# GpSimd takes over three elementwise steps of a two-way decaying mix in front of a feed-forward kernel

## The chip, the cores and the metric

The kernel runs on one core of one Trainium2 chip. Its time is the device time of one execution, in microseconds (us). A core has five engines that run their own instruction queues beside each other and meet through semaphores: TensorE (PE, with its weight loads as PEld), VectorE (DVE), ScalarE (ACT), GpSimd (POOL) and SyncE (SP), which here only issues DMAs.

## The reference, cut to what matters

x and fside are 4 x 1024 (time) x 1024 (channels), float32. fside serves as k and v, x as r:

```
decay = exp(-exp(w)) * (0.5 + 0.5 * tf)          # one per batch and channel
ek, ekv = exp(min(k, 30)), exp(min(k, 30)) * v
a = a * decay + ek or ekv                        # over time, forward (nf, df) and reversed (nb, db)
euk = exp(min(u + k, 30))
num, den = nf + nb - ekv + euk * v, df + db - ek + euk
m = sigmoid(r) * num / max(den, 1e-8) * (0.8 + 0.2 * tf)
h = m @ W1.T                                     # 1024 -> 4096
a = gelu(clip(round(h / 0.1)) * 0.1)
out = x + a @ W2.T                               # 4096 -> 1024
```

## The kernel before, in words

The work is 8 blocks (`BLOCKS`): 4 batches of two time halves of 512 steps (`T`), the later half first. A block's mix is 8 tiles of 128 channels x 512 steps, numbered `g` over all blocks; `tile_of(g)` says whether it is of a late half. A block's feed-forward has a hidden stage of 8 steps (W1, quantise, gelu) and an output stage of 8 results of 128 channels (W2). Values go to TensorE as two float16 parts, a high part (ScalarE copies) and a low part (value minus high part). In block 0 the low parts are written by `mix_lo` (line 1034); later blocks have an operand scheme of their own (`operand_sums`, `operands_lo`), which the change does not touch.

Order of the work. The tiles of block 0 come first, alone (line 1124). Then, while TensorE does block n's feed-forward, the other engines make the tiles of block n+1, interleaved by hand: each engine's program is one fixed list, and `part(p, g)` (line 1015) is a quarter of a tile on VectorE. Tile g and tile g+2 share buffers (index `g % 2`).

A tile on VectorE: `weigh` makes ek * v. `forward` does two scans (NUM and DEN), `backward` two reversed ones into EK and EKV. `sums` adds: DEN + EK (line 992), the bonus terms (995, 998), NUM + EKV (1001, semaphore `s_num1`), the floor (1003), two 1-column carries, NUM + V (1009) and the gate (1012, `s_gate`). The reciprocal of the tile before (ScalarE's logarithm and exponential, two Newton steps and line 947) is woven into the scans.

A tile of a late half lacks the earlier half's state, so it is made directly: the exponent's argument is min(VP, 30) + RAMP * ln(decay) over the earlier half VP, ScalarE exponentiates and sums it, and `weigh` multiplies it by VP and sums (line 926, `s_dot`). The argument is `prefix_argument` (line 911): a one-input multiply (915) and a two-input instruction (918), both on VectorE, for tile g+1 after tile g's backward scans.

GpSimd only issues DMAs (line 446): in block 0's tiles one cast of a W1 piece per step to a float16 copy in memory (449, once the tile's R has landed) and every second step one of W2 (451); in block 0's hidden stage four more of W2, in its output stage three copies a step, each behind a semaphore of TensorE's progress. SyncE issues everything else in one list: `load_tile` loads VP, V and R, where VP waits for `s_dot` and V for `s_gate` of the tile two before; `ring_load` fills the ring of weights, where the first sixteen wait for the casts.

ScalarE waits for the argument (`s_arg`) in `exps`, for the floor in `reciprocal`, for the scaled output in `mix_hi`.

Of the kernel before, what the change touches and what calls it, by code (L numbers as in the profile page):

```python
# [6 lines left out]
ALU = mybir.AluOpType  # L7
# [8 lines left out]
CLIP = 30.0  # L16
# [17 lines left out]
def adaln_ffn_kernel(nc, x, fside, cond, w, u, w1, w2, out):  # L34
# [18 lines left out]
    with ExitStack() as ctx:  # L53
# [3 lines left out]
        def sem(name):  # L57
            return ctx.enter_context(nc.semaphore(name))
# [96 lines left out]
        s_vp = [sem(f"s_vp{k}") for k in range(2)]  # L155
        s_argr = sem("s_argr")
        s_arg = sem("s_arg")
        s_ekp = sem("s_ekp")
        s_dot = sem("s_dot")
        s_ekx = sem("s_ekx")  # L160
# [63 lines left out]
        def tile_of(g):  # L224

            n, t = g // CT, g % CT
            return n % BLOCKS // 2, n % 2 == 0, (t % 2) * KH + t // 2, CT * (n // 2) + t
# [216 lines left out]

        @block.gpsimd
        def _(pool):
            for s in range(STEPS):
                pool.wait_ge(s_r[s % 2], 16 * (s // 2 + 1))
                pool.dma_start(w1_half[s], w1_full[s]).then_inc(s_w1cast[s], 16)
                if s % 2 == 1:  # L450
                    pool.dma_start(w2_half[s // 2], w2_full[s // 2]).then_inc(s_w2cast[s // 2], 16)
            for d in range(DT // 2, DT):
                pool.wait_ge(s_h0, FPS * (d - 1))
                pool.dma_start(w2_half[d], w2_full[d]).then_inc(s_w2cast[d], 16)
            for s in range(STEPS):
                pool.wait_ge(s_y, 2 + s)
                pool.wait_ge(s_w1cast[s], 16)
                for r, h, k in ((WP1, 0, 0), (WP2, 0, 1), (WP4, 1, 1)):
                    pool.dma_start(w1s[s][:, r, :, :], w1_quads[s][:, h, :, k, :]).then_inc(s_w1copy[s], 16)
            for d in range(DT):  # L460
                pool.wait_ge(s_w2cast[d], 16)
            for s in range(STEPS):
                pool.wait_ge(s_w1copy[s], 16 * 3)

        @block.tensor
        def _(pe):
# [409 lines left out]
        def _(dve):  # L876
# [31 lines left out]
                dve.wait_ge(s_lndec, B + 1)  # L908
                dve.wait_ge(s_setup, 6 + B)

            def prefix_argument(g):
                b, late, c, pg = tile_of(g)
                if late:
                    dve.wait_ge(s_ramp, 3)
                    v.tensor_scalar(EKP[:, :], RAMP[:, :], lndec[:, b, c:c + 1], None, ALU.mult).then_inc(s_argr, 1)
                    dve.wait_ge(s_vp[pg % 2], 16 * (pg // 2 + 1))
                    dve.wait_ge(s_argr, pg + 1)
                    v.scalar_tensor_tensor(out=EKP[:, :], in0=VP[:, pg % 2, :], scalar=CLIP, in1=EKP[:, :],  # L918
                                           op0=ALU.min, op1=ALU.add).then_inc(s_arg, 1)

            def weigh(g):
                b, late, c, pg = tile_of(g)
                k = g % 2
# [64 lines left out]
            def sums(g):  # L988
                b, late, c, pg = tile_of(g)
                k = g % 2  # L990
                dve.wait_ge(s_dbwd, g + 1)
                v.tensor_tensor(DEN[:, k, :], DEN[:, k, :], EK[:, k, 1:T + 1], ALU.add).then_inc(s_den1, 1)
                dve.wait_ge(s_bon, g + 1)
                dve.wait_ge(s_vsq, g + 1)
                v.scalar_tensor_tensor(out=V[:, k, :], in0=BON[:, k, :], scalar=EXP_CLIP, in1=V[:, k, :],
                                       op0=ALU.min, op1=ALU.mult).then_inc(s_vbon, 1)
                dve.wait_ge(s_den1, g + 1)
                v.scalar_tensor_tensor(out=DEN[:, k, :], in0=BON[:, k, :], scalar=EXP_CLIP, in1=DEN[:, k, :],
                                       op0=ALU.min, op1=ALU.add).then_inc(s_den2, 1)
                dve.wait_ge(s_nbwd, g + 1)  # L1000
                v.tensor_tensor(NUM[:, k, :], NUM[:, k, :], EKV[:, k, 1:T + 1], ALU.add).then_inc(s_num1, 1)
                dve.wait_ge(s_den2, g + 1)
                v.tensor_scalar(DEN[:, k, :], DEN[:, k, :], DEN_MIN, None, ALU.max).then_inc(s_den3, 1)
                if late:
                    v.tensor_copy(carry[:, 0, c:c + 1], EKV[:, k, 0:1]).then_inc(s_carry, 1)
                    v.tensor_copy(carry[:, 1, c:c + 1], EK[:, k, 0:1]).then_inc(s_carry, 1)
                dve.wait_ge(s_num1, g + 1)
                dve.wait_ge(s_vbon, g + 1)
                v.tensor_tensor(NUM[:, k, :], NUM[:, k, :], V[:, k, :], ALU.add).then_inc(s_num2, 1)  # L1009
                dve.wait_ge(s_num2, g + 1)  # L1010
                dve.wait_ge(s_tanh, g + 1)
                v.scalar_tensor_tensor(out=NUM[:, k, :], in0=R[:, k, :], scalar=1.0, in1=NUM[:, k, :],
                                       op0=ALU.add, op1=ALU.mult).then_inc(s_gate, 1)

            def part(p, g):

                last = g - 1 if g % CT else None
                if p == 0:
                    weigh(g)
                if p == 1:  # L1020
                    forward(g, last)
                if p == 2:
                    backward(g, last)
                    if g % CT < CT - 1:
                        prefix_argument(g + 1)
                if p == 3:
                    sums(g)

            def divide(g):
                newton(g, 0)  # L1030
                newton(g, 1)
                mixed_out(g)

            def mix_lo(g):
                c = tile_of(g)[2]
                dve.wait_ge(s_mixhi, g + 1)
                v.tensor_tensor(mix0[:, c, 1, :], m_st[:, m_slot(g), g % 2, :], mix0[:, c, 0, :],  # L1037
                                ALU.subtract).then_inc(s_mix, 1)

            def operand_sums(n, q):  # L1040
                g, at = CT * n + 2 * q, KH * (n - 1) + q
# [78 lines left out]
                                       op0=ALU.mult, op1=ALU.not_equal, accum_out=bad[:, at:at + 1]).then_inc(s_chk, 1)  # L1120

            factors()
            prefix_argument(0)
            for t in range(CT):
                for p in range(4):
                    part(p, t)
                    if p == 3 and t > 0:
                        mix_lo(t - 1)
            divide(CT - 1)
            mix_lo(CT - 1)  # L1130

            def hidden_block0(g0):
                for s in range(STEPS):
# [17 lines left out]
            def hidden_block(n, nxt, g0):  # L1151
                for s in range(STEPS):
                    if nxt:
                        if s == 0:
                            prefix_argument(g0)
                        elif s % 2 == 0:
                            part(3, g0 + s // 2 - 1)
                        else:
                            part(1, g0 + s // 2)
                    if s >= 2:  # L1160
                        act_lo(n, s - 2, 1)
                    if s >= 1:
                        quantise22(n, s - 1)
                    if nxt:
                        part(0 if s % 2 == 0 else 2, g0 + s // 2)
                    seed_u4(n, s)
                    if s >= 1:
                        act_lo(n, s - 1, 0)
# [83 lines left out]
            def general_block(m):  # L1252
                n = BLOCKS + m
                for t in range(CT):
                    g = CT * n + t
                    prefix_argument(g)
                    weigh(g)
                    forward(g, None)
                    backward(g, None)
# [54 lines left out]
```

## Time and profile before

| | us |
|---|---|
| median of 3 runs (1815.62 to 1816.57) | 1816.48 |
| the profiled execution | 1813.9 |
| its span | 1811.6 |
| TensorE busy | 1699.9 (94%) |
| VectorE busy | 1279.5 (71%) |
| ScalarE busy | 1043.5 (58%) |
| GpSimd busy | 24.6 (1%) |

Busy time is an average over stages that have different limits; the table of stretches below shows it by stage. A wait counts the idle time of an engine in front of an instruction and names what came last. Idle time of an engine that is not the bottleneck costs nothing.

### The profile page before, as it was taken

To read this page: it belongs to the slowest core of one execution; us is meant where nothing else is said; L and a number is where in the kernel's file an instruction comes from. 1 tells how busy PE (TensorE), PEld (TensorE's weight loads), DVE (VectorE), ACT (ScalarE), POOL (GpSimd) and SP (SyncE) were. 2 spreads that over 40 slices of the span, in tenths; PEclk is the share of its full clock that TensorE was granted. 3 is DMA by queue.
4 is the path that set the end of the run, shared out by engine and by line. 5 is a ranking of instruction groups with operands and counts; after the bars stand their busy time and mean duration, and the time that the engine had idled before them with its cause. 6 is when DMAs were issued, how large, how long until landed. Compare 5 with 4: busy or idle time off the path is not lost. (4 is left out here: it accounts for less than half of the span.)

```text
span 1811.6 us, 27451 instructions
## 1 busy us (share of the span) xinstructions
PE 1699.9 (94%) x10882; PEld 1067.0 (59%) x10882; DVE 1279.5 (71%) x2008; ACT 1043.5 (58%) x1422; POOL 24.6 (1%) x44
## 2 busy tenths in 40 slices
PE   1459999999999999999999999999999999999998
PEld 0124434687448854588447864488545874478643
DVE  8988885878866786779866777678966687633211
ACT  5458843687437863498526874388634885255300
POOL 0000021000000000000000000000000000000000
PEclk9679999999999999999999999999999999999999
DMA  8747785665546644655446545466445654365442
GB/s 239 178 128 204 253 286 198 204 198 181 162 147 204 195 139 155 198 191 202 162 133 203 187 158 174 144 217 204 156 144 192 195 180 152 120 194 158 145 129 82
DMA packets 109238, 321.16 MB, mean 177 GB/s; under 512 B 12720, under 2 KB 12720, under 8 KB 108592
## 3 DMA queue, kind: packets, MB, share of 16 engines
q1 hardware_dynamic: 106416, 296.28, 50.1%
q0 software_dynamic: 2688, 23.07, 5.5%
q8 instruction: 87, 1.43, 0.3%
q14 instruction: 47, 0.39, 0.1%
HBM read 310.91 MB, written 48.23 MB: 198 GB/s over the span
## 5 line engine op out<-in xcount | busy, mean ns | idle before, releaser
L562 PE MATMUL ps<-act,w_ring 128*128 128x512 f16 x4096 | 890.7, 380 | 4.4 <-DVE y_out L1111 4.4
L506 PE MATMUL ps<-mo,w_ring 128*128 128x256 f16 x6272 | 690.6, 273 | 11.0 <-ACT ps L706 6.1
L562 PEld LDWEIGHTS ps<-act,w_ring 128*128 128x128 f16 x4096 | 401.4, 98 | 485.7 <-issue 8.8
L506 PEld LDWEIGHTS ps<-mo,w_ring 128*128 128x128 f16 x6272 | 612.5, 98 | 90.1 <-issue 7.8
L1102 DVE SCALAR_TENSOR_TENSOR act<-a,act 128x1024 f16<-128x1024 f32 x128 | 156.2, 1221 | 134.7 <-ACT act L755 134.7
L1111 DVE SCALAR_TENSOR_TENSOR y_out<-ps,x_in 128x512 f32<-128x512 f32 x64 | 44.1, 690 | 175.1 <-PE ps L562 107.3
L763 ACT ACTIVATE q<-chk_full 128x1024 int8<-128x1024 f32 x64 | 67.0, 1047 | 144.5 <-DMA chk_full<-in_w_dram 144.5
L749 ACT ACTIVATE a<-q 128x1024 f32<-128x1024 int16 x128 | 135.3, 1057 | 14.6 <-DVE act L1102 10.3
L755 ACT ACTIVATE act<-a 128x1024 f16<-128x1024 f32 x128 | 134.2, 1049 | 0.9
L483 PE MATMUL ps<-mo,w_ring 128*128 128x512 f16 x128 | 42.6, 509 | 89.3 <-DVE mo L1037 89.3
L1119 DVE SCALAR_TENSOR_TENSOR chk_full<-q,chk_full 128x1024 f32<-128x1024 int8 x64 | 78.1, 1220 | 43.8 <-ACT q L763 43.8
L696 ACT ACTIVATE mo<-a 128x1024 f16<-128x1024 f32 x28 | 29.6, 1057 | 128.8 <-DVE a L1048 128.8
L650 ACT ACTIVATE EK<-V 128x512 f32<-128x512 f32 x64 | 39.9, 623 | 109.6 <-DMA V<-in_fside_dram 109.3
L646 ACT ACTIVATE EKP<-EKP 128x512 f32<-128x512 f32 x32 | 20.2, 631 | 133.7 <-DVE EKP L918 133.5
L1085 DVE SCALAR_TENSOR_TENSOR ps<-sp,ps 128x512 f32<-128x512 f32 x56 | 38.8, 692 | 73.7 <-PE ps L506 66.9
L483 PEld LDWEIGHTS ps<-mo,w_ring 128*128 128x128 f16 x128 | 15.4, 125 | 116.0 <-issue 55.8
L496 PE MATMUL ps<-mo,w_ring 128*128 128x512 f16 x384 | 83.0, 379 | 0.0
L670 ACT ACT_TABLE_LOAD x64 | 82.1, 1283 | 1.1
L643 ACT ACT_TABLE_LOAD x64 | 82.1, 1283 | 1.1
L733 ACT ACTIVATE q<-ps 128x512 int16<-128x512 f32 x56 | 33.3, 594 | 85.6 <-PE ps L506 85.6
L978 DVE TENSOR_TENSOR_SCAN EK<-EK,decay 128x512 f32<-128x512 f32 x64 | 81.7, 1277 | 0.1
L983 DVE TENSOR_TENSOR_SCAN EKV<-EKV,decay 128x512 f32<-128x512 f32 x64 | 81.6, 1276 | 0.0
(94 smaller groups left out, 1461.1 us busy)
## 6 DMA issues: line engine op xcount, KB each, us to landing
w_ring<-w1s SPq DMA_DIRECT2D x168, 512.0 KB, 3.7
w_ring<-w_half SPq DMA_DIRECT2D x144, 512.0 KB, 4.2
chk_full<-in_w_dram SPq DMA_DIRECT2D x64, 512.0 KB, 4.6
V<-in_fside_dram SPq DMA_DIRECT2D x64, 256.0 KB, 4.7
R<-in_x_dram SPq DMA_DIRECT2D x64, 256.0 KB, 4.8
w_half<-in_w_dram POOLq DMA_DIRECT2D x16, 1024.0 KB, 7.9
x_in<-in_x_dram SPq DMA_DIRECT2D x64, 256.0 KB, 5.3
out_dram<-y_out SPq DMA_DIRECT2D x64, 256.0 KB, 4.8
```

The source lines that it names most:

```text
L496: mm = pe.matmul(bank[4 * (s % 2) + j][:, :], w1_ring[:, k, f, c, :], mix0[:, c, p, :], start=(c == 0 and p == 0), stop=(c == CT - 1 and p ...
L506: mm = pe.matmul(dst[:, f, :], wp_ring[:, k, r, f, q, :], mo[:, op, q, p, :], start=(fresh and f == 0 and q == 0 and p == 0), stop=(q == K ...
L562: mm = pe.matmul(y_ps[y][:, :], w2_ring[:, k, f, :], act[:, a, p, :], start=(a == 0 and p == 0), stop=(a == FT - 1 and p == 1))
L643: sc.preload_act_table_set(EXP_SET)
L670: sc.activation(R[:, g % 2, :], R[:, g % 2, :], ACT.Tanh, scale=0.5).then_inc(s_tanh, 1)
L749: sc.activation(a32[:, 2 * h:2 * h + 2, :], q16[:, s % 2, 2 * h:2 * h + 2, :], ACT.Gelu_apprx_tanh, scale=QSTEP).then_inc(s_gelu, 1)
L755: sc.activation(act[:, f:f + 2, 0, :], a32[:, 2 * h:2 * h + 2, :], ACT.Copy, scale=ACT_SCALE).then_inc(s_ahi, 1)
L763: sc.activation(chk_i8, chk_full[:, :], ACT.Copy, scale=W_SCALE).then_inc(s_chki8, 1)
L978: v.tensor_tensor_scan(EK[:, k, 0:T][:, ::-1], EK[:, k, 0:T][:, ::-1], dec(b, c), EK[:, k, T:T + 1], ALU.add, ALU.mult).then_inc(s_dbwd, 1)
L983: v.tensor_tensor_scan(EKV[:, k, 0:T][:, ::-1], EKV[:, k, 0:T][:, ::-1], dec(b, c), EKV[:, k, T:T + 1], ALU.add, ALU.mult).then_inc(s_nbwd, 1)
L1102: v.scalar_tensor_tensor(out=act[:, f:f + 2, 1, :], in0=a32[:, 2 * h:2 * h + 2, :], scalar=ACT_SCALE, in1=act[:, f:f + 2, 0, :], op0=ALU.m ...
L1119: v.scalar_tensor_tensor(out=chk_full[:, :], in0=chk_i8, scalar=1.0 / W_SCALE, in1=chk_full[:, :], op0=ALU.mult, op1=ALU.not_equal, accum_ ...
```

## The change

Three steps move from VectorE's list to GpSimd's.

1. The exponent's argument of each late tile. On GpSimd it is three instructions instead of two: the multiply, the minimum into the tile's BON buffer (which is free until ScalarE's exponential fills it), and the sum. It now waits for `s_dot` of the late tile before and for `s_gate` of the tile two before.
2. The add of the backward numerator, NUM + EKV, of every tile, right behind `s_nbwd`.
3. The low part of block 0's tiles (`mix_lo`).

They stand between GpSimd's DMA issues as the diff shows. The fallback path behind the last If gets them too; it is not taken with these inputs.

```diff
@@ GpSimd's program
+            def prefix_argument(g):
+                b, late, c, pg = tile_of(g)
+                if late:
+                    pool.wait_ge(s_ramp, 3)
+                    pool.wait_ge(s_lndec, B + 1)
+                    if pg > 0:
+                        pool.wait_ge(s_dot, pg)
+                    pl.tensor_scalar(EKP[:, :], RAMP[:, :], lndec[:, b, c:c + 1], None, ALU.mult).then_inc(s_argr, 1)
+                    pool.wait_ge(s_vp[pg % 2], 16 * (pg // 2 + 1))
+                    pool.wait_ge(s_argr, pg + 1)
+                    if g >= 2:
+                        pool.wait_ge(s_gate, g - 1)
+                    pl.tensor_scalar(BON[:, g % 2, :], VP[:, pg % 2, :], CLIP, None, ALU.min).then_inc(s_kp, 1)
+                    pool.wait_ge(s_kp, pg + 1)
+                    pl.tensor_tensor(EKP[:, :], BON[:, g % 2, :], EKP[:, :], ALU.add).then_inc(s_arg, 1)
+
+            def mix_lo(g):
+                c = tile_of(g)[2]
+                pool.wait_ge(s_mixhi, g + 1)
+                pl.tensor_tensor(mix0[:, c, 1, :], m_st[:, m_slot(g), g % 2, :], mix0[:, c, 0, :],
+                                ALU.subtract).then_inc(s_mix, 1)
+
+            def add_backward(g):
+                k = g % 2
+                pool.wait_ge(s_nbwd, g + 1)
+                pl.tensor_tensor(NUM[:, k, :], NUM[:, k, :], EKV[:, k, 1:T + 1], ALU.add).then_inc(s_num1, 1)
+
+            prefix_argument(0)
             for s in range(STEPS):
                 pool.wait_ge(s_r[s % 2], 16 * (s // 2 + 1))
                 pool.dma_start(w1_half[s], w1_full[s]).then_inc(s_w1cast[s], 16)
+                if s + 1 < CT:
+                    prefix_argument(s + 1)
                 if s % 2 == 1:
                     pool.dma_start(w2_half[s // 2], w2_full[s // 2]).then_inc(s_w2cast[s // 2], 16)
+                add_backward(s)
+                if s > 0:
+                    mix_lo(s - 1)
+            mix_lo(CT - 1)
             for d in range(DT // 2, DT):
                 pool.wait_ge(s_h0, FPS * (d - 1))
                 pool.dma_start(w2_half[d], w2_full[d]).then_inc(s_w2cast[d], 16)
+                add_backward(CT + d - DT // 2)
             for s in range(STEPS):
...
+                if s % 2 == 1:
+                    add_backward(CT + CT // 2 + s // 2)
+            for g in range(2 * CT, CT * BLOCKS):
+                if g % CT == 0 and g > 2 * CT:
+                    add_backward(g - 1)
+                prefix_argument(g)
+                if g % CT > 0:
+                    add_backward(g - 1)
+            add_backward(CT * BLOCKS - 1)
...
@@ VectorE's program: prefix_argument, mix_lo and all calls of them are gone, and in sums
-                dve.wait_ge(s_nbwd, g + 1)
-                v.tensor_tensor(NUM[:, k, :], NUM[:, k, :], EKV[:, k, 1:T + 1], ALU.add).then_inc(s_num1, 1)
```

## Rows read from the trace of the kernel before

**Rows 1.** stretches: length, busy us of PE, PEld, DVE, ACT, POOL; clock, DMA share, GB/s.

```profile
40.00:80.00 40.00, 15.75 (x44) 5.37 (x42) 39.31 (x70) 18.64 (x34) 2.44 (x5) 0.68 0.80 178
...
600.00:800.00 200.00, 199.68 (x1330) 129.82 (x1328) 146.33 (x221) 121.93 (x164) 0.00 (x0) 1.00 0.55 177
```

**Rows 2.** waits up to 134 us: who waited for whom, total us, times, longest.

```profile
POOL w_half L449 <- DMA R<-in_x_dram: 93.1, 8, 19.4
PE ps L483 <- DVE mo L1037: 89.3, 7, 37.8
...
ACT EKP L646 <- DVE EKP L918: 46.0, 8, 7.1
```

**Rows 3.** VectorE, one tile of the front: start us, us, engine, line, operation.

```profile
99.71 0.69 DVE L937 TENSOR_TENSOR DEN<-DEN,RCP 128x512 f32<-128x512 f32 x1
...
102.09 1.28 DVE L983 TENSOR_TENSOR_SCAN EKV<-EKV,decay 128x512 f32<-128x512 f32 x1
103.29 0.73 DVE L947 SCALAR_TENSOR_TENSOR m_st<-NUM,ogain_neg,RCP 128x512 f32<-128x512 f32 x1
103.93 0.48 DVE L915 TENSOR_SCALAR EKP<-RAMP,lndec 128x512 f32<-128x512 f32 x1
104.52 0.69 DVE L918 SCALAR_TENSOR_TENSOR EKP<-VP,EKP 128x512 f32<-128x512 f32 x1
105.13 0.68 DVE L992 TENSOR_TENSOR DEN<-DEN,EK 128x512 f32<-128x512 f32 x1
...
106.93 0.69 DVE L1001 TENSOR_TENSOR NUM<-NUM,EKV 128x512 f32<-128x512 f32 x1
107.53 0.42 DVE L1003 TENSOR_SCALAR DEN<-DEN 128x512 f32<-128x512 f32 x1
...
108.00 0.68 DVE L1009 TENSOR_TENSOR NUM<-NUM,V 128x512 f32<-128x512 f32 x1
...
109.32 0.69 DVE L1037 TENSOR_TENSOR mo<-m_st,mo 128x512 f16<-128x512 f32 x1
109.92 0.69 DVE L926 SCALAR_TENSOR_TENSOR EKV<-EKP,VP 128x512 f32<-128x512 f32 x1
...
114.18 0.69 DVE L937 TENSOR_TENSOR DEN<-DEN,RCP 128x512 f32<-128x512 f32 x1
```

**Rows 4.** all engines, the first tile's argument and the first casts.

```profile
7.44 0.65 POOL L449 DMA_DIRECT2D w_half<-in_w_dram  x1 [6.99 <-DMA R<-in_x_dram]
...
8.85 0.49 DVE L915 TENSOR_SCALAR EKP<-RAMP,lndec 128x512 f32<-128x512 f32 x1
...
9.65 0.51 POOL L449 DMA_DIRECT2D w_half<-in_w_dram  x1 [1.56 <-DMA R<-in_x_dram]
...
10.18 0.63 ACT L646 ACTIVATE EKP<-EKP 128x512 f32<-128x512 f32 x1 [0.94 <-DVE EKP L918]
...
15.89 0.45 SPq L315 DMA_DIRECT2D VP<-in_fside_dram  x1
```

**Rows 5.** VectorE, the last two low parts of the front.

```profile
122.60 0.69 DVE L1037 TENSOR_TENSOR mo<-m_st,mo 128x512 f16<-128x512 f32 x1
...
126.77 0.69 DVE L1037 TENSOR_TENSOR mo<-m_st,mo 128x512 f16<-128x512 f32 x1 [0.70 <-ACT mo L681]
```

**Rows 6.** TensorE, first matmul group behind the first result of block 0.

```profile
246.87 15.34 PE L562 MATMUL ps<-act,w_ring 128*128 128x512 f16 x57 [4.44 <-DVE y_out L1111]
```

**Rows 7.** waits of TensorE after the front.

```profile
PE ps L506 <- ACT ps L706: 6.1, 7, 1.3
PE ps L506 <- DVE mo L1054: 4.5, 4, 1.6
```

**Rows 8.** VectorE, a hidden stage of block 1.

```profile
395.51 1.23 DVE L1102 SCALAR_TENSOR_TENSOR act<-a,act 128x1024 f16<-128x1024 f32 x1 [3.75 <-ACT act L755]
...
419.96 1.22 DVE L1102 SCALAR_TENSOR_TENSOR act<-a,act 128x1024 f16<-128x1024 f32 x1 [3.75 <-ACT act L755]
```

**Rows 9.** waits of VectorE after the front.

```profile
DVE y_out L1111 <- PE ps L562: 102.6, 20, 12.0
```

More of the change, by code:

```diff
@@ L157, in adaln_ffn_kernel @@
         s_arg = sem("s_arg")
+        s_kp = sem("s_kp")
         s_ekp = sem("s_ekp")
@@ L446, in _ @@
         def _(pool):
+            pl = nc.gpsimd
+            def prefix_argument(g):
[23 more added lines that the diff above has]
+            prefix_argument(0)
             for s in range(STEPS):
@@ L463, in _ @@
                 pool.wait_ge(s_w1copy[s], 16 * 3)
+            pool.wait_ge(s_flag, 1)
+            needs_general = pool.value_load(flag[0:1, 0:1], min_val=0, max_val=1)
+            with pool.If(needs_general > 0):
+                for g in range(CT * BLOCKS, 2 * CT * BLOCKS):
+                    prefix_argument(g)
+                    add_backward(g)
         @block.tensor
@@ L909, in factors @@
                 dve.wait_ge(s_setup, 6 + B)
[L911 to L919, printed above, removed]
             def weigh(g):
@@ L1023, in part @@
                     backward(g, last)
-                    if g % CT < CT - 1:
-                        prefix_argument(g + 1)
                 if p == 3:
@@ L1032, in divide @@
                 mixed_out(g)
[L1034 to L1038, printed above, removed]
             def operand_sums(n, q):
@@ L1122, in _ @@
             factors()
-            prefix_argument(0)
             for t in range(CT):
@@ L1126, in _ @@
                     part(p, t)
-                    if p == 3 and t > 0:
-                        mix_lo(t - 1)
             divide(CT - 1)
-            mix_lo(CT - 1)
             def hidden_block0(g0):
@@ L1153, in hidden_block @@
                     if nxt:
-                        if s == 0:
-                            prefix_argument(g0)
-                        elif s % 2 == 0:
+                        if s % 2 == 1:
+                            part(1, g0 + s // 2)
+                        elif s > 0:
                             part(3, g0 + s // 2 - 1)
-                        else:
-                            part(1, g0 + s // 2)
                     if s >= 2:
@@ L1255, in general_block @@
                     g = CT * n + t
-                    prefix_argument(g)
                     weigh(g)
```

## The prediction, made before the changed kernel was run

> **What bounds the kernel now.** I read the table of stretches first [rows 1]. In the steady part (600 to 800 us) TensorE is busy 199.7 of 200 us; between 40 and 80 us it is busy 15.8 of 40 while VectorE is busy 39.3. So there are two kernels in one: a front that ends near 127 us, in which VectorE paces the eight tiles of block 0, and the long rest, in which TensorE does. The waits of the front say the same [rows 2]: TensorE waited 89.3 us for the low part that VectorE writes on line 1037. ScalarE waited 46.0 us for the exponent's argument, so ScalarE is not the pace. GpSimd waited 93.1 us for loads and is otherwise empty. After the front all waits of TensorE sum to 15.0 us (4.4 + 6.1 + 4.5) [rows 6, 7]. Whatever the change does to the time, it does in the front, or by making VectorE late enough later on to open new gaps in TensorE.
>
> VectorE's queue of one tile is the unit of the sum [rows 3]. Line 937 starts at 99.71 and again at 114.18: a tile takes 14.47 us, back to back. I count start to start, since the ends overlap the next start by some 0.08 us.
>
> **Removed from VectorE, per tile.** The argument (lines 915 and 918): 103.93 to 105.13, 1.20 us. The backward numerator's add (line 1001): 106.93 to 107.53, 0.60 us. The low part (line 1037): 109.32 to 109.92, 0.60 us. In all 2.40 of 14.47 us.
>
> In the front that is 7 arguments (tiles 1 to 7), 8 adds and 6 low parts (tiles 0 to 5; tile 6's lay in VectorE's wait for ScalarE at the end, and tile 7's ends the front): 8.4 + 4.8 + 3.6 = 16.8 us removed.
>
> **Moved to the ends of the front.** Argument 0 runs from 8.85 until ScalarE takes it at 10.18 [rows 4]; as three instructions instead of two, on GpSimd, it ends some 0.8 us later. Low part 7 is the last thing before TensorE's sixteen final matmuls of the stage [rows 5]: 126.77 plus 0.69 us now, some 0.5 us longer on a slower engine. Low part 6, which now waits its turn until 122.60, can be made as soon as ScalarE has copied the high part, but TensorE then only has its sixteen matmuls done earlier and waits for tile 7; no gain.
>
> **Price of an instruction on GpSimd.** The trace has no GpSimd instruction that reads a tile; its only work is issuing DMAs at 0.49 us. Lower bound: what VectorE takes, 0.48 us for one input and 0.60 for two. Upper bound: the slowest row of this shape, the scan, 1.20 us start to start [rows 3]. For one input I take 0.48, for two 1.20, because GpSimd has to fetch two tiles and no row suggests it does so as fast as the engine built for it. By the Trainium skill (GPSIMD Engine Reference, Elementwise — side-by-side cycle accounting) an add of 2048 elements takes 1.96 times as long on GpSimd; as an estimate that would be 1.18 us here, and the sum would be the same.
>
> **Does that time lie beside VectorE's?** This decides the sign. Nothing in the trace shows both engines reading tiles at once, so both ends stand. What rows do show: VectorE's one-input instruction on line 1003 (0.42 us) handles the same 512 elements that the two-input ones take 0.68 us for [rows 3]. An engine that goes about twice as fast with one input uses both of its read paths for it; with two inputs both are taken as well. Nearly everything in its queue (scans, products, sums) has two tile inputs. If GpSimd has no path of its own, its reads have to take VectorE's. I therefore put the likelier case at "they take turns", each GpSimd instruction holding back the VectorE one behind it for its whole length.
>
> The Trainium skill (SBUF — State Buffer, Who interferes with whom) has this as a rule: a VectorE instruction with two SBUF inputs contends with a GpSimd instruction that reads SBUF, and the second to issue waits in full. No run so far shows it; by it the sum is the one for turns below, without it the one for side by side.
>
> Taking turns, the front changes by: arguments 7 x (0.48 + 0.48 + 1.20 - 1.20) = +6.7; argument 0 +0.8; adds 8 x (1.20 - 0.60) = +4.8; low parts 6 x 0.60 = +3.6; low part 6 now competes with tile 7's sums, +1.2; low part 7 +0.5. Together +17.6 us. From it goes what VectorE can do while GpSimd holds the path: the small memsets and carry copies and the accumulator read, some 0.5 us a tile, 3.5 us in seven tiles. Front: +14.1 us.
>
> **Waits that are added.** Line 1009 now waits for GpSimd's add. The backward scan ends near 103.3 (line 947 starts behind it at 103.29), line 1009 starts at 108.00, or 106.2 with the argument and the add gone: 2.9 us of cover for a 1.20 us instruction. It does not bind unless the add takes over 2.8 us. Behind it on VectorE stand lines 1012 and the next tile's product. The argument is needed only by the next tile's product, 10 us later, so its chain of three is covered.
>
> **GpSimd's own queue.** Each weight cast now stands behind an argument, an add and a low part, so casts 1 to 7 start up to 10 us later relative to R's landing. The sync engine's ring loads wait for them in order, and tile loads stand behind those. The first casts now start near 11 us instead of 7.44 and 19 instead of 9.65 [rows 4]; VP of tile 2 would then be issued near 20 instead of 15.9 and is needed after 22. I cost this at nothing; if the cover is gone it is a few us once, in tiles 1 and 2.
>
> **After the front.** In block 0's hidden stage VectorE is nearly full, and its lateness shows once: TensorE waits 4.4 us for the first result on line 1111 [rows 6]. Two adds (tiles 10 and 11) lie in the unbroken run before it: 2 x 0.60 less if side by side, 2 x 0.60 more if in turns, so +1.2. In the hidden stages of later blocks VectorE waits 3.75 us for ScalarE in every two steps (24.5 us) [rows 8]; the extra per late tile in turns is 0.96 + 0.60 = 1.6 us, which fits. TensorE's other waits stay [rows 7]: 6.1 us are for ScalarE's copy, which the change does not touch. The output stages have VectorE waiting for TensorE for 102.6 us in all [rows 9]. The other 24 arguments and most of the 56 later adds lie where TensorE does not wait for VectorE, and gain or lose nothing.
>
> **Sum.** The profiled run took 1813.9 us (span 1811.6). Plus 14.1 and 1.2 is 1829.2. The median of the runs lies 2.6 us above the profiled run, so 1831.8 us.
>
> **Rivals.**
> 1. Side by side (ends faster). GpSimd reads without holding VectorE back. Front -16.8 + 0.8 + 0.5 = -15.5; block 0 -1.2. 1797.2, with the offset 1799.8 us. For it: GpSimd's DMA issues lie in VectorE's full queue without a stretched instruction beside them; against it: those do not read tiles, and the pair 0.42 against 0.68. It decides from any price up to 2.8 us, since covered work costs nothing.
> 2. In turns, but GpSimd is as quick as VectorE (0.48 and 0.60). Arguments 7 x 0.36 = +2.5, ends +1.3, low part 6 +0.6, less 3.5 of small work: about +1. 1817 us; a half-way overlap of slow instructions ends in the same place (1808 to 1824).
> 3. A two-input instruction takes over 2.4 us when it has to fight for the path. Then line 1009 waits, the extra per late tile passes the 3.75 us of slack, and TensorE gets gaps in 24 late tiles: over 1850 us. Nothing in the rows speaks for it.
> The change does what it says: the instructions are really gone from VectorE's queue, so "nothing happens" is only rival 2.
>
> **Chances.** Turns 0.52, side by side 0.30, rival 2 0.10, rival 3 0.08. What this kernel's measurement can tell from no change is 0.2%, 3.6 us. Faster: 0.30 plus a part of rival 2, 0.33; within: 0.09; slower: 0.58. The range takes in side by side at its near half (1799) and ends where turns with every instruction in full, 17.6 in the front, and some late gaps end (1843). The likeliest case alone runs from 1822 to 1843.
>
> **What would show each step.** VectorE's rows in the front: two-input instructions that stretch from 0.68 us beside a GpSimd one (turns), or keep their 0.68 (side by side). The tile's period, 14.47 us now: 16 with turns, 12.1 side by side. Mean of the GpSimd add: 1.2 us. Line 1009's wait for GpSimd: none. TensorE's wait on line 483: 89.3 us growing to some 103, or falling to 74. TensorE's wait for line 1111: 5.6 or 3.2 us. I am wrong if VectorE's instructions keep their lengths, or if the time moves outside the front.

## The result and the profile after

| | before | after |
|---|---|---|
| median (range, runs), us | 1816.05 (1814.51 to 1816.57, 4) | 1842.42 (1842.04 to 1842.82, 4) |
| ratio, 95% interval | | 1.0147 [1.0129, 1.0164] |
| profiled execution / its span | 1813.9 / 1811.6 | 1842.8 / 1840.9 |
| TensorE / VectorE / ScalarE / GpSimd busy | 1699.9 / 1279.5 / 1043.5 / 24.6 | 1708.8 / 1281.3 / 1045.9 / 325.4 |

The median of before now takes in a fourth run. The changed kernel is slower, by 26.4 us in the medians and by 29.3 us in the spans of the two profiled executions (the one of before lay 2.1 us under its median). VectorE gave away 136 of its 2008 instructions and is no less busy: 1281.3 against 1279.5 us. Its remaining instructions became longer.

I read first where TensorE's stages start, since their distance is the loss of each stage. The front's end is the first matmul on line 550 (before: line 496); a block's output stage begins with its unbroken run of 448 matmuls on line 616 (before: 562).

| start of | before | after | later by | added here |
|---|---|---|---|---|
| block 0's hidden stage | 131.76 | 142.55 | 10.8 | 10.8 |
| block 1's output stage | 447.72 | 463.50 | 15.8 | 5.0 |
| block 7's output stage | 1707.65 | 1733.49 | 25.8 | 10.0 |
| VectorE's last instruction | 1806.34 | 1832.18 | 25.8 | 0 |
| end of the span | 1811.6 | 1840.9 | 29.3 | 3.5 |

So four places carry it: the front 10.8, the way from block 0 to block 1 5.0, blocks 1 to 7 10.0, and what lies behind the last instruction 3.5 us.

**The front.** The two stretches after, in the columns of [rows 1]:

```profile
40.00:80.00 40.00, 17.59 (x48) 6.07 (x48) 39.41 (x56) 20.12 (x30) 27.42 (x18) 0.79 0.74 165
600.00:800.00 200.00, 199.21 (x1322) 128.94 (x1320) 150.46 (x217) 120.41 (x160) 25.29 (x14) 1.00 0.54 172
```

VectorE is still full in the front (39.4 of 40 us) with 56 instructions in place of 70, and TensorE now loses something in the steady part too. TensorE's waits over the whole run, against [rows 2, 7]:

```profile
PE ps L537 <- POOL mo L469: 53.2, 6, 10.5
PE ps L537 <- DMA w_ring<-w_half: 44.4, 1, 44.4
PE ps L560 <- DVE mo L1088: 9.4, 6, 2.4
PE ps L560 <- DVE y_out L1145: 7.2, 4, 4.9
```

The wait of this stage is now 53.2 + 44.4 = 97.6 us in place of 89.3. The first wait ended at 44.41 with the ring's load; the first low part had been written at 41.13 (line 469, 39.80 plus 1.33). So 3.3 us of it are the late weight casts. They cost nothing in the end, since the next groups of matmuls wait for low parts again. The same tile-long piece of VectorE's list as in [rows 3], from line 975 to line 975:

```profile
90.04 1.06 DVE L975 TENSOR_TENSOR EKV<-EK,V 128x512 f32<-128x512 f32 x1
...
92.40 1.56 DVE L1005 TENSOR_TENSOR_SCAN DEN<-decay,pre_d,EK 128x512 f32<-128x512 f32 x1
93.91 1.76 DVE L981 TENSOR_TENSOR DEN<-DEN,RCP 128x512 f32<-128x512 f32 x1
...
101.12 1.20 DVE L1045 TENSOR_SCALAR DEN<-DEN 128x512 f32<-128x512 f32 x1
...
102.37 1.52 DVE L1051 TENSOR_TENSOR NUM<-NUM,V 128x512 f32<-128x512 f32 x1
...
105.59 1.06 DVE L975 TENSOR_TENSOR EKV<-EK,V 128x512 f32<-128x512 f32 x1
```

and GpSimd in the same stretch:

```profile
89.87 1.56 POOL L457 TENSOR_SCALAR EKP<-RAMP,lndec 128x512 f32<-128x512 f32 x1 [1.55 <-DVE EKV L970]
91.59 2.18 POOL L462 TENSOR_SCALAR BON<-VP 128x512 f32<-128x512 f32 x1
93.85 1.26 POOL L464 TENSOR_TENSOR EKP<-BON,EKP 128x512 f32<-128x512 f32 x1
...
98.73 3.31 POOL L475 TENSOR_TENSOR NUM<-NUM,EKV 128x512 f32<-128x512 f32 x1 [3.07 <-DVE EKV L1027]
102.00 1.33 POOL L469 TENSOR_TENSOR mo<-m_st,mo 128x512 f16<-128x512 f32 x1
```

Put side by side, each GpSimd instruction has one stretched VectorE instruction beside it: 975 takes 1.06 instead of 0.69 us, 1005 1.56 instead of 1.26, 981 1.76 instead of 0.69, 1045 1.20 instead of 0.42, 1051 1.52 instead of 0.68. The two beside one-input instructions (457, 462) lost 0.37 and 0.30 (and line 462 itself took 2.18 us instead of the 1.49 it takes alone), the three beside two-input ones (464, 475, 469) 1.07, 0.78 and 0.84: together 3.36 us. Removed were 2.40, and 0.11 us is a new gap in front of line 1045. The period is 105.59 - 90.04 = 15.55 us, 1.08 more than in [rows 3]; 3.36 + 0.11 - 2.40 = 1.07. From the first tile's line 975 (14.91, before: line 931 at 12.00) to the eighth's (121.15, before: 110.99) the changed kernel loses 7.25 us: 0.74 in the first step and 1.08 in each of the six others. The last tile and its low part add 0.6. The rest of the front's 10.8 is its beginning:

```profile
8.38 1.57 POOL L457 TENSOR_SCALAR EKP<-RAMP,lndec 128x512 f32<-128x512 f32 x1 [7.94 <-DVE lndec L961]
10.11 1.49 POOL L462 TENSOR_SCALAR BON<-VP 128x512 f32<-128x512 f32 x1 [0.16 <-POOL EKP L457]
11.68 1.26 POOL L464 TENSOR_TENSOR EKP<-BON,EKP 128x512 f32<-128x512 f32 x1
```

The first argument ends at 12.94 us, against 10.14 before although it starts earlier [rows 4], and VectorE's first product starts at 13.84 instead of 10.93: 2.9 us later. These rows also give GpSimd's prices with VectorE idle: 1.57 and 1.49 us for one input, 1.26 for two.

**From block 0 to block 1.** GpSimd after:

```profile
293.64 1.51 POOL L475 TENSOR_TENSOR NUM<-NUM,EKV 128x512 f32<-128x512 f32 x1 [7.72 <-DVE EKV L1027]
295.09 4.12 POOL L497 DMA_DIRECT2D w1s<-w_half  x6
```

and before, the last of these copies:

```profile
284.74 2.05 POOL L459 DMA_DIRECT2D w1s<-w_half  x3 [4.86 <-PE ps L562]
```

Six copies of weights stood 7.72 us behind tile 14's add, which waited for VectorE's backward scan. SyncE's ring load of those weights was issued at 303.61 instead of 289.86, and the loads of V, R and x_in stand behind it in SyncE's list. VectorE felt it (first row), then TensorE (the other two):

```profile
309.28 0.69 DVE L1145 SCALAR_TENSOR_TENSOR y_out<-ps,x_in 128x512 f32<-128x512 f32 x1 [15.08 <-DMA x_in<-in_x_dram]
...
345.71 1.44 PE L560 MATMUL ps<-mo,w_ring 128*128 128x256 f16 x6 [4.88 <-DVE y_out L1145]
349.57 43.42 PE L560 MATMUL ps<-mo,w_ring 128*128 128x256 f16 x378 [2.42 <-DVE mo L1088]
```

Before, TensorE waited 1.59 and 1.28 us at the same seam, the passage from one block's output stage to the next block's hidden stage (at 335.03 and 339.59), so the seam's longer waits are 4.4 of the 5.0 us. During the first of them the granted clock falls to 0.50, the lower of its two levels (1.2 GHz), and stays there from 343.4 to 353.7.

The stall behind the first result of block 0, 4.44 us in [rows 6], is now 3.21. A second one, of 1.20 us, stands at 326.86, in front of the block's eighth result. It belongs to the copies' delay, since the run that undoes that delay (e4 below) doesn't have it.

**From block to block.** From one output stage's start to the next the six stretches add 2.3, 2.1, 1.8, 1.8, 1.9 and 0.3 us. GpSimd makes two arguments in the first, third and fifth, six in the second and fourth, and none in the last, so the drift stands where arguments are made. I followed it in the first, at the end of block 1's output stage. The chain is long. Before:

```profile
503.53 0.43 SPq L315 DMA_DIRECT2D VP<-in_fside_dram  x1
...
507.31 0.69 DVE L918 SCALAR_TENSOR_TENSOR EKP<-VP,EKP 128x512 f32<-128x512 f32 x1 [7.43 <-DMA VP<-in_fside_dram]
...
508.03 0.63 ACT L646 ACTIVATE EKP<-EKP 128x512 f32<-128x512 f32 x1 [17.58 <-DVE EKP L918]
...
515.59 1.23 DVE L1119 SCALAR_TENSOR_TENSOR chk_full<-q,chk_full 128x1024 f32<-128x1024 int8 x1 [1.12 <-ACT q L763]
...
518.17 0.43 SPq L329 DMA_DIRECT2D x_in<-in_x_dram  x1
...
524.06 0.69 DVE L1111 SCALAR_TENSOR_TENSOR y_out<-ps,x_in 128x512 f32<-128x512 f32 x1 [4.24 <-DMA x_in<-in_x_dram]
```

After:

```profile
519.31 0.43 SPq L316 DMA_DIRECT2D VP<-in_fside_dram  x1
...
523.46 1.49 POOL L462 TENSOR_SCALAR BON<-VP 128x512 f32<-128x512 f32 x1 [15.25 <-DMA VP<-in_fside_dram]
525.03 1.27 POOL L464 TENSOR_TENSOR EKP<-BON,EKP 128x512 f32<-128x512 f32 x1
...
526.34 0.63 ACT L700 ACTIVATE EKP<-EKP 128x512 f32<-128x512 f32 x1 [17.00 <-POOL EKP L464]
...
533.10 1.23 DVE L1153 SCALAR_TENSOR_TENSOR chk_full<-q,chk_full 128x1024 f32<-128x1024 int8 x1 [2.61 <-ACT q L817]
...
535.68 0.43 SPq L330 DMA_DIRECT2D x_in<-in_x_dram  x1
...
541.68 0.69 DVE L1145 SCALAR_TENSOR_TENSOR y_out<-ps,x_in 128x512 f32<-128x512 f32 x1 [4.35 <-DMA x_in<-in_x_dram]
```

VP's load is issued 15.8 us later in both, which is the lateness that was there already. From its landing to ScalarE's exponential it is 0.72 us before and 2.88 after. Of this 2.16 us more, ScalarE had 0.87 to spare, which it spent waiting for the floor before. Its list carries the rest on to its next quantising step, VectorE's check waits 2.61 instead of 1.12 us for that, SyncE's load of the next piece waits for the check, x_in stands behind it, and y_out waits for x_in: 17.6 us later where VP was 15.8 later. What TensorE then does:

```profile
561.21 0.82 PE L560 MATMUL ps<-mo,w_ring 128*128 128x256 f16 x6 [0.85 <-DVE y_out L1145]
564.00 93.79 PE L560 MATMUL ps<-mo,w_ring 128*128 128x256 f16 x842 [1.98 <-DVE mo L1088]
```

From one output stage's start to the next (block 1's to block 2's) the stretches are, before and then after, in the columns of [rows 1]:

```profile
447.70:658.70 211.00, 208.89 (x1411) 137.57 (x1410) 157.32 (x245) 130.99 (x177) 0.00 (x0) 1.00 0.53 173
```

```profile
463.50:676.70 213.20, 210.37 (x1411) 138.29 (x1409) 153.85 (x232) 131.08 (x177) 22.91 (x15) 0.99 0.54 171
...
566.00:572.00 6.00, 6.00 (x44) 4.67 (x43) 2.73 (x5) 4.92 (x7) 0.00 (x0) 0.78 1.00 377
```

Of the 2.2 us that this block adds, 0.7 are TensorE's longer idle time (2.83 for 2.11 us) and 1.5 are the same 1411 matmuls taking longer. The last row shows where: behind the two waits of 0.85 and 1.98 us the granted clock is 0.78 of full speed in the mean over 6 us, in which TensorE is never idle. For 3.4 us (565.3 to 568.7) it stands at its lower level, 1.2 GHz. The same happens at the seams behind blocks 3 and 5, and at none behind blocks 2, 4 and 6. It isn't a second price, though. In e1 below, which keeps the arguments on GpSimd, the clock does not fall here and the stretch adds 2.0 us all the same (212.95 us, TensorE busy 208.99), now all of it idle time:

```profile
557.26 3.28 PE L536 MATMUL ps<-mo,w_ring 128*128 128x256 f16 x26 [1.99 <-DVE mo L1072]
561.56 89.24 PE L536 MATMUL ps<-mo,w_ring 128*128 128x256 f16 x816 [1.03 <-ACT ps L736]
```

The slower matmuls take the place of the third wait. Over the whole run TensorE is busy 8.9 us longer for the same instructions, at a mean granted clock of 0.976 instead of 0.982; how much of that is lost time isn't shown.

In the stretches with six arguments most of the loss lies in the hidden stage. From block 2's output stage to block 3's TensorE waits 0.62 us at the seam (before: 0.32) and 0.39 and 0.42 us for VectorE's quantising step (line 1129), and the same 1411 matmuls take 209.30 instead of 208.48 us at full clock. The chain of these was not followed.

There is a rival at the seam. GpSimd's add stands in its list behind an argument that waits for VP, and VectorE waits for the add: 2.90 us at 502.36 and 5.36 us at 527.39 (line 1051), and likewise in blocks 3 and 5. e1 has these arguments and no add on GpSimd, and the first stretch adds 2.0 there as against 2.3. So it is the argument and not the add that carries most of the drift.

**Behind the last instruction.** VectorE's last instruction (line 1278) starts at 1832.18 and the span ends 8.7 us later; before it was 5.3 us (1806.34 to 1811.6).

### The profile page after: what moved, and what is told of

It is laid out like the page before. It is cut to its first block and busy times, and to the rows that moved or that the text cites. A ratio compares the mean times of both kernels' runs of the same rounds, so it can differ in the third digit from the quotient of the medians.

```text
span 1840.9 us, 27520 instructions
## 1 busy us (share of the span) xinstructions
PE 1708.8 (93%) x10882; PEld 1069.7 (58%) x10882; DVE 1281.3 (70%) x1872; ACT 1045.9 (57%) x1422; POOL 325.4 (18%) x212
## 5 line engine op out<-in xcount | busy, mean ns | idle before, releaser
L560 PE MATMUL ps<-mo,w_ring 128*128 128x256 f16 x6272 | 699.1, 274 | 19.7 <-DVE mo L1088 9.4
L560 PEld LDWEIGHTS ps<-mo,w_ring 128*128 128x128 f16 x6272 | 615.4, 98 | 105.1 <-issue 15.3
L475 POOL TENSOR_TENSOR NUM<-NUM,EKV 128x512 f32<-128x512 f32 x64 | 134.1, 2095 | 869.8 <-DVE EKV L1027 869.8
L1136 DVE SCALAR_TENSOR_TENSOR act<-a,act 128x1024 f16<-128x1024 f32 x128 | 162.4, 1269 | 137.9 <-ACT act L809 137.9
L537 PE MATMUL ps<-mo,w_ring 128*128 128x512 f16 x128 | 45.0, 531 | 97.7 <-POOL mo L469 53.2
L462 POOL TENSOR_SCALAR BON<-VP 128x512 f32<-128x512 f32 x32 | 62.1, 1942 | 171.2 <-DMA VP<-in_fside_dram 169.7
L457 POOL TENSOR_SCALAR EKP<-RAMP,lndec 128x512 f32<-128x512 f32 x32 | 52.8, 1651 | 194.3 <-DVE EKV L970 186.3
```

The source lines that it names most:

```text
L462: pl.tensor_scalar(BON[:, g % 2, :], VP[:, pg % 2, :], CLIP, None, ALU.min).then_inc(s_kp, 1)
L475: pl.tensor_tensor(NUM[:, k, :], NUM[:, k, :], EKV[:, k, 1:T + 1], ALU.add).then_inc(s_num1, 1)
L537: mm = pe.matmul(bank[4 * s + j][:, :], w1_ring[:, slots[2 * s + j // 2], j % 2, c, :], mix0[:, c, p, :], start=(t == 0 and p == 0), stop= ...
L560: mm = pe.matmul(dst[:, f, :], wp_ring[:, k, r, f, q, :], mo[:, op, q, p, :], start=(fresh and f == 0 and q == 0 and p == 0), stop=(q == K ...
L1136: v.scalar_tensor_tensor(out=act[:, f:f + 2, 1, :], in0=a32[:, 2 * h:2 * h + 2, :], scalar=ACT_SCALE, in1=act[:, f:f + 2, 0, :], op0=ALU.m ...
```

## The experiments

Each ratio is against runs of the kernel before that were taken along with it (medians 1815.4 to 1815.5, for the changed kernel 1816.05). "Front" is the start of block 0's hidden stage less 131.76.

| run | median, us | ratio, 95% | front | block 1 / 7 later by | tail, us |
|---|---|---|---|---|---|
| changed kernel | 1842.42 | 1.0147 [1.0129, 1.0164] | +10.8 | 15.8 / 25.8 | 8.7 |
| e1 argument only | 1832.96 | 1.0100 [1.0083, 1.0117] | +6.2 | 9.0 / 18.0 | 5.6 |
| e2 additions only | 1820.92 | 1.0028 [1.0017, 1.0039] | +3.6 | 7.3 / 9.6 | 5.5 |
| e3 low parts only | 1815.25 | 0.9996 [0.9986, 1.0006] | +1.2 | 4.1 / 5.0 | 5.0 |
| e4 copies first | 1837.91 | 1.0120 [1.0103, 1.0137] | +10.9 | 11.1 / 20.7 | 8.6 |
| e5 before + reading probe | 1836.76 | 1.0116 [1.0100, 1.0131] | +21.0 | 24.0 / 24.6 | 5.4 |
| e6 before + writing probe | 1816.42 | 1.0005 [0.9996, 1.0015] | +0.5 | 1.8 / 3.0 | 5.1 |
| e7 branch on VectorE | 1840.25 | 1.0132 [1.0117, 1.0148] | +10.2 | 16.9 / 26.6 | 5.1 |
| e8 ScalarE's product | 1811.33 | 0.9979 [0.9970, 0.9988] | -3.4 | -4.3 / -3.5 | 5.3 |
| e9 late arguments back | 1829.50 | 1.0077 [1.0060, 1.0094] | +10.7 | 13.3 / 15.6 | 5.4 |

The block columns come from single profiled executions, and the stall behind block 0's first result alone moves them by some 3 us. It also shows a pattern: 4.4 to 7.8 us in the six kernels in which VectorE makes the adds (before, e1, e3, e5, e6, e8), 2.2 to 3.3 in the five in which GpSimd does (changed, e2, e4, e7, e9). The front and the drift from block 1 to 7 are steadier.

**e1, e2, e3: one part at a time.** The changed kernel with two of its three moves undone.

```
e1   (GpSimd)   prefix_argument kept; mix_lo and add_backward back on VectorE
e2   (GpSimd)   add_backward kept; prefix_argument and mix_lo back on VectorE
e3   (GpSimd)   mix_lo kept; the other two back on VectorE, and no branch at GpSimd's end
```

> Only the exponent's argument is on GpSimd; the add and the low part are on VectorE. Theory (a GpSimd instruction that reads tiles holds back the VectorE instruction behind it): VectorE's product on line L975 and its scan and product behind it stretch by 0.37, 0.31 and 1.07 us a tile, 1.75 against 1.20 saved, +0.55 us in 7 tiles, and the first argument comes 3.5 us later: front +7.4 us. With the tail's 3.4 us and some later gaps 1827 to 1835 us. Rival (VectorE is late because it waits for GpSimd's result): the argument is needed only 10 us later, so nothing stretches, front -8.4 + 3.5 = -5 us, about 1815 us with the tail.

> Only the add of the backward numerator is on GpSimd. Theory: GpSimd gets at its tiles only when VectorE leaves a gap, and then the one-input floor instruction stretches from 0.42 to 1.20 us: +0.78 + 0.11 - 0.60 = +0.3 us a tile, front +2.3 us; in block 0's output stage the adds stand before the copies of weights, +5.6 us; tail +3.4 us. 1826 to 1834 us. Rival (waits): VectorE idles in front of the line that adds V, and the rows there show it.

> Only the low part of block 0 is on GpSimd, and there is no If in GpSimd's program. Theory: +0.83 - 0.60 = +0.23 us a tile in six, +0.5 at the end: front +2 us, nothing later, no longer tail: 1817 to 1820 us. Rival (side by side): front -3.6 + 0.5 = -3 us, 1813 us.

Measured: 1832.96, 1820.92 and 1815.25 us. The fronts add up (6.2 + 3.6 + 1.2 = 11.0 against 10.8). The argument is the dearest part: it brings two one-input instructions, a two-input one and the late start. VectorE in e1, a tile:

```profile
87.33 1.06 DVE L951 TENSOR_TENSOR EKV<-EK,V 128x512 f32<-128x512 f32 x1
...
91.20 1.76 DVE L957 TENSOR_TENSOR DEN<-DEN,RCP 128x512 f32<-128x512 f32 x1
...
102.36 1.06 DVE L951 TENSOR_TENSOR EKV<-EK,V 128x512 f32<-128x512 f32 x1
```

The same three are stretched by the same amounts (line 951 by 0.37, the scan 1.56 instead of 1.26, line 957 by 1.07); the period is 15.03 us. They are the argument's. e1 also keeps 9.0 of the 10.0 us that blocks 1 to 7 add; e2 has 2.3 and e3 0.9 of it.

e2 came out 5 us under its expectation. Its front lost more than expected (3.6 against 2.3 us), the way to block 1 less (3.7 against 5.6), and the 3.4 us behind the last instruction did not come (5.5 against 5.3 us before). Nor is it the floor that stretches in e2 (0.43 us) but the multiply of the argument, a one-input instruction too, which VectorE still makes there: 1.32 instead of 0.48 us (line 935 at 90.72). e1's tail did not come either (5.6 us).

e3 came out under its expectation as well and is indistinguishable from before: GpSimd takes the low part while VectorE runs a scan, which goes from 1.28 to 1.99 us, so 0.71 is paid for 0.60 removed.

**e4: the weight copies ahead of tiles 14 and 15's adds.**

```
-                if s % 2 == 1:
+                if s in (1, 3):
                     add_backward(CT + CT // 2 + s // 2)
+            add_backward(2 * CT - 2)
+            add_backward(2 * CT - 1)
```

> The changed kernel with the adds of tiles 14 and 15 moved behind GpSimd's last weight copies. Theory: in block 0's output stage the copies stood behind an add that waits for VectorE, SyncE's list stood behind the copies, and results and tile loads behind SyncE: 15.1 us of VectorE's wait for x_in, seen by TensorE as 5.6 us more of gaps. They go: 1835 to 1838 us. Rival (those gaps are VectorE's stretched instructions): no change, 1842 us.

1837.91 us, 4.5 less than the changed kernel. Block 1's output stage starts 4.7 us earlier (458.82), block 7's 5.1 us. TensorE waits 0.24 and 3.04 us at the seam instead of 4.88 and 2.42, and not at all in front of block 0's eighth result. That settles the second place: the copies' delay was worth 4.5 to 5 us, and it was only an order in one list. (The two ratios' intervals overlap; all four runs of e4, 1834.4 to 1838.8, lie under all four of the changed kernel.)

**e5, e6: is it reading?** Both put five idle instructions per tile of the front beside the unchanged kernel's VectorE, at the places where the change has its own. In e5 they read (two one-input, three two-input, all into scratch), in e6 they are memsets of the same tile, which read nothing.

```
+            def extra(two_inputs):
+                pool.wait_ge(s_scr, done[0])
e5+              pl.tensor_tensor(SCR, RAMP, RAMP, ALU.add)  or  pl.tensor_scalar(SCR, RAMP, CLIP, None, ALU.min)
e6+              pl.memset(SCR, 1.0)
```

> The kernel before, with five more GpSimd instructions per tile of block 0 at the places of the change (two with one input, three with two inputs, all from a constant tile into an unused buffer); VectorE keeps all its instructions and nobody waits for the new ones. Theory (reads on GpSimd hold VectorE back): VectorE's instructions stretch by about 3.4 us a tile, front +20 to +25 us, 1836 to 1842 us. Rival (what costs is waiting for GpSimd's results): nothing stretches, 1816 us.

> As the run that adds reads, but the five extra instructions are memsets of the same size: they write a tile and read none. Theory (it is the reading that collides): no stretch beside VectorE's two-input instructions, 1816 to 1818 us. Rival (any GpSimd instruction on tiles collides): +10 us or more.

e5 took 1836.76 us, e6 1816.42. Three of the five stretched rows of VectorE in e5:

```profile
92.14 1.41 DVE L1039 SCALAR_TENSOR_TENSOR NUM<-R,NUM 128x512 f32<-128x512 f32 x1
...
97.43 1.57 DVE L988 TENSOR_TENSOR_SCAN DEN<-decay,pre_d,EK 128x512 f32<-128x512 f32 x1
98.93 1.52 DVE L964 TENSOR_TENSOR DEN<-DEN,RCP 128x512 f32<-128x512 f32 x1
```

Stretched are line 1039 by 0.72, 988 by 0.31, 964 by 0.83, and 942 by 0.78 and 958 by 0.29: 2.93 us a tile, and seven tiles of that are 20.5 of the front's 21.0. In e6 the same rows keep their length beside the memsets:

```profile
99.10 1.26 DVE L988 TENSOR_TENSOR_SCAN DEN<-decay,pre_d,EK 128x512 f32<-128x512 f32 x1
100.30 0.69 DVE L964 TENSOR_TENSOR DEN<-DEN,RCP 128x512 f32<-128x512 f32 x1
```

```profile
96.79 1.32 POOL L460 MEMSET chk_full<- 128x512 f32 x2 [0.38 <-DVE EKV L953]
```

The waits and semaphores of the two probes are the same. The memsets are shorter, five of them some 2.6 us a tile; had they held VectorE back for that length, the front would be 18 us later, as an estimate, and it is 0.5 later. So no dependence, queue or semaphore stretches VectorE's rows; GpSimd's reading does. The Trainium skill (SBUF — State Buffer, Who interferes with whom) says the same of two-input VectorE instructions, and that GpSimd instructions which only write don't contend: both agree with these runs. Its "fully blocks" comes near for GpSimd's two-input instructions (0.71 to 1.07 us lost beside 1.26 us of work), and does not hold for its one-input ones (0.29 to 0.37 lost beside 1.5).

**e7: where does the tail come from?** GpSimd's branch, which holds the general path's arguments and adds and is never taken, is removed, and VectorE's own branch, which is there in every kernel, makes them as before.

```
-            pool.wait_ge(s_flag, 1)
-            needs_general = pool.value_load(flag[0:1, 0:1], min_val=0, max_val=1)
-            with pool.If(needs_general > 0):
-                ...
```

> The changed kernel with the never-taken fallback of the three steps in VectorE's If and none in GpSimd's program. Theory: the 3.4 us between the last VectorE instruction and the end of the span that the changed kernel has more than before (8.7 against 5.3 us) belong to GpSimd's branch; they go: 1839 us. Rival: the tail has another cause and stays, 1842.4 us.

1840.25 us; the tail is 5.1 us, 3.6 less. The spans differ by 2.9 us, as block 7 is 0.8 later here, and the medians by 2.2 (the ratios' intervals overlap, the two sets of runs don't). So the tail belongs to the branch, although it does nothing. Having a branch on GpSimd is not enough: e1, e2 and e9, whose branch holds only the arguments or only the adds, end after 5.4 to 5.6 us. Why the whole body costs over 3 us and either half next to nothing is not shown.

**e8: the multiply on ScalarE.** The kernel before, with the one-input product of tiles 1 to 7 made by ScalarE, which waited 46.0 us for it [rows 2].

```
+            def product(g):
+                act_e.wait_ge(s_dot, pg)
+                sc.activation(EKP[:, :], RAMP[:, :], ACT.Copy, scale=lndec[:, b, c:c + 1]).then_inc(s_argr, 1)
```

> The kernel before, with the product RAMP * ln(decay) of tiles 1 to 7 made by ScalarE, which waits 46 us in the front, in place of VectorE (one 0.48 us instruction per tile, 0.58 us start to start). Theory (ScalarE does not slow VectorE): front 7 x 0.58 = 4.1 us shorter, 1812 us. Rival (the product comes late, as ScalarE is behind): same or slower, 1816 to 1819 us.

1811.33 us: faster than both kernels, by 4.1 us (0.2%). The front is 3.4 us shorter. VectorE after its reciprocal's last step goes straight on to the sum; the tile's period is 13.88 us (line 936 from 91.93 to 105.81), 0.59 less than in [rows 3], and nothing in it is stretched:

```profile
99.77 0.72 DVE L957 SCALAR_TENSOR_TENSOR m_st<-NUM,ogain_neg,RCP 128x512 f32<-128x512 f32 x1
100.41 0.68 DVE L928 SCALAR_TENSOR_TENSOR EKP<-VP,EKP 128x512 f32<-128x512 f32 x1
...
105.81 0.69 DVE L936 SCALAR_TENSOR_TENSOR EKV<-EKP,VP 128x512 f32<-128x512 f32 x1
```

**e9: the drift of the later blocks.** The changed kernel with the arguments of blocks 2, 4 and 6 on VectorE again.

```
             for g in range(2 * CT, CT * BLOCKS):
-                prefix_argument(g)
+    (VectorE)   prefix_argument(g), two instructions, in its old place, for g >= 2 * CT
```

> The changed kernel, with the argument of the tiles of blocks 2, 4 and 6 made on VectorE again, in its old two instructions and its old place; block 0's arguments, the low parts and all additions stay on GpSimd. Theory (the later blocks' drift of 10 us is the price of the late arguments: the argument alone on GpSimd showed 9.0 of it, the additions alone 2.3): the front stays 10 to 11 us late, block 1's product as late as in the changed kernel (463 us), but from there to block 7 it loses at most 3 us instead of 10, and the tail shrinks by 1 us or more since the branch's body is smaller: 1829 to 1834 us. Rival: the drift comes from the additions' waits and the later clock dips, and stays: 1840 to 1843 us. If the tail's 3.4 us come from the size of the branch's body, it is between 5.5 and 8.7 us here.

1829.50 us, 12.9 less than the changed kernel. The front is as late as there (142.49), blocks 1 to 7 add 2.3 us instead of 10.0, and the tail is 5.4 us. At the seam followed above, VP's landing and ScalarE's exponential are 0.72 us apart again:

```profile
520.97 0.69 DVE L970 SCALAR_TENSOR_TENSOR EKP<-VP,EKP 128x512 f32<-128x512 f32 x1 [6.93 <-DMA VP<-in_fside_dram]
...
521.69 0.63 ACT L698 ACTIVATE EKP<-EKP 128x512 f32<-128x512 f32 x1 [17.28 <-DVE EKP L970]
```

and VectorE's check waits 1.12 us for ScalarE as it did before the change (line 1163 at 528.77); TensorE is busy 208.88 us in that block, as before. So the late arguments carry 7.7 of the 10.0 us. They also bring VectorE's wait for the add, which is gone in e9 too; that this is not what costs is e1's to say, as above. The spans of the two profiled executions differ by 13.5 us; the rest of that is the tail (3.3 us, with only the adds in the branch) and 2.4 us between the front and block 1's output stage, where block 2's first arguments are made, and where single executions differ by as much.

## Why the prediction was right in sign and short in size

1832 us was forecast, in turns, with a range to 1843; 1842.4 was measured, at its edge. The sign and the mechanism of the front held. But of 29.3 us only 10.8 lie in the front. The prediction had named time that moves outside the front as a sign of being wrong, and by that sign its account of the rest was wrong: 18.5 us came from places that it costed at 1.2. That the time still fell inside the range is in part luck. Step by step:

- **"In turns" is the case.** Two-input instructions stretched beside GpSimd's (0.69 to 1.76 us), and e5 against e6 shows that it is the reading. The period was to be 16 us with turns and is 15.55. Side by side (12.1 us), rival 1, is out.
- **The price of an instruction.** Two inputs: 1.20 taken, 1.26 measured alone, and 0.78 to 1.07 of it lost by VectorE. One input: 0.48 taken, 1.49 to 1.57 measured, but only 0.30 to 0.37 lost. The row I leaned on for one input was VectorE's own lower bound. For VectorE both errors are on the same side: 4.56 us a tile less the 0.5 allowed for small work was forecast, 3.36 measured. The front came out 10.8 us late where 14.1 was forecast. The 0.5 us a tile of small work that was to go on beside GpSimd was not measured by itself.
- **Argument 0: 0.8 us forecast, 2.9 measured.** Here the one-input price counts in full, since nothing runs beside it. It hides a part of the overestimate above.
- **The add's mean of 1.2 us is wrong: 2.10,** 3.31 in the front. It does not run slowly; it doesn't get in. Line 475 was released by the scan at 98.6 and VectorE's next four instructions followed one another without a stretch until the short gap in front of line 1045 (101.12), where GpSimd began and VectorE waited. So its release took three times its length, and still line 1051 did not wait in the front, as forecast (though not for the forecast's reason, a limit of 2.8 us: the stretched line 1045 moved line 1051 back with it). In later blocks it waited six times, 24.7 us in all, the longest 5.4, each time because the add stood behind an argument that waited for VP. This is rival 3's place; e1, which has no such wait, drifts by 9.0 us all the same.
- **TensorE's wait on the low parts: 103 forecast, 97.6 measured,** of which 3.3 are for the ring's load.
- **Behind block 0's first result: 5.6 forecast, 3.21 measured.** Here the sign was wrong. 3.2 is what the prediction gave for side by side, yet line 1045 is stretched to 1.20 us in this stage too (at 239.61). All five kernels with the adds on GpSimd have this stall at 2.2 to 3.3 us; why it shortens was not followed.
- **"GpSimd's own queue costs nothing" failed.** I followed it for the casts, where it was right in the outcome (the first group of matmuls waited 3.3 us for them, the front's end did not move), and not for the weight copies of block 0's output stage, which are the same queue 170 us later. 5 us (e4 recovered 4.5).
- **"After the front nothing" failed.** I compared VectorE's extra work (1.6 us a tile) with its idle 3.75 us in the hidden stages [rows 8], and that slack held only for the most part: in block 3's hidden stage TensorE waited 0.39 and 0.42 us for VectorE. The output stages were waved through with VectorE's 102.6 us of waiting [rows 9]. But the argument is there not VectorE's work but a link between a load and ScalarE, made when the load lands: its latency of 2.9 instead of 0.7 us passes through ScalarE, VectorE and SyncE. 10.0 us, of which e9 shows 7.7. A wait of an engine says that it has time, not that what it waits for has.
- **The tail, 3.5 us in the spans, was not in the sum.** e7 shows that it is GpSimd's branch.

The sum of the forecast was +15.3 us in the profiled executions, the measured one +28.9: -3.3 in the front, -1.2 for the forecast at block 0's first result, +5.0 for the whole way to block 1, +10.0 and +3.5 for the places costed at nothing, 14.0 in the spans; the missing 13.6 us are that less 0.4, by which the time around the span shrank (2.3 to 1.9). The medians differ by less, since the profiled run of before was below its median and that of after was not.

## What to carry to other kernels

Moving an instruction from a full VectorE to GpSimd need not take its time off VectorE: here each two-input instruction moved saved 0.60 us and cost 0.7 to 1.1 us in VectorE's neighbour, so the break-even is lost before any queue is counted. The one-input multiply of the argument saved 0.59 and cost 0.37, so moved alone it might have gained 0.2 us a tile; no run tried it. ScalarE made the same product with no stretched row beside it, and the tile became 0.59 us shorter. Before an instruction is moved, follow what its new engine's list already carries through all stages, not only in the one that is to gain. And ask of each moved step whether it is work or a link between a load and another engine, since a link's latency is paid even where every engine has idle time.

## What the runs showed of the hardware that was not expected

- On GpSimd a one-input instruction of 128x512 float32 (1.49 to 1.57 us alone) is slower than a two-input one (1.26 us, 1.15 for the last low part); on VectorE it is the other way round (0.42 to 0.48 against 0.68).
- GpSimd's two-input instruction waited through four VectorE instructions issued back to back and got in at the first gap of a semaphore: 3.31 us for 1.26 us of work. VectorE's instruction there, a one-input one, was stretched too, 0.42 to 1.20 us.
- GpSimd's memset of the same tile takes 0.52 us and costs VectorE nothing (e6).
- A short spell of the lower clock behind a seam need not cost anything of its own: with it the stretch added 2.3 us, without it (e1, e4) 2.0 and 2.1, as TensorE waits there anyway.
- A branch that is never taken, at the end of GpSimd's list, made the span some 3.5 us longer behind the last instruction (8.7 against 5.1 to 5.3 us) when its body held arguments and adds for 64 tiles, and 0.1 to 0.3 us when it held one of the two.
